# GpSimd takes the last two exponentials of a routed layer, and the first expert tile is prepared earlier

## The chip, the cores and the metric

The kernel runs on one core of a Trainium2 chip. The metric is the device time in microseconds (us) of the whole program, as the median of a few executions.

## What is computed

The input is two sequences of 2048 tokens, 256 numbers each. Two layers follow each other, both behind a layer normalisation and both added to their input:

```python
x = x + attn(layernorm(x))   # linear attention with decay, 4 heads, scanned in chunks
x = x + ffn(layernorm(x))    # 8 experts, each token goes to its 2 best
# inside ffn
logits = einsum('bsd,ed->bse', x, gate_w)
probs = softmax(logits)
topk_probs, topk_idx = top_k(probs, 2)
h = gelu(w1[expert] @ x + b1[expert])
y = w2[expert] @ h + b2[expert]
out = sum(y * topk_probs)
```

The softmax is computed as e to the logits less the largest, divided by its sum. The first step of that, for the last two of 16 chunks, is what the change touches.

## The kernel before

Each engine has one instruction stream, written out by hand, and they meet through semaphores. Work comes in two stages.

**Stage one** goes over 16 chunks of 128 tokens of both sequences at once (`m` = 0 to 15, `NCH` = 16). A step `n` handles several chunks, each at its own lag: loads and statistics of chunk n, attention of n-1 and n-2, residual sum and second normalisation of n-3, the experts' scores of n-4, and the routing of n-5. The routing of a chunk m on VectorE is:

- `logits(m)` copies the scores from PSUM; `largest(m)` takes the maxima and writes the shifted logits (`shifted`, 128 partitions by 16 numbers, semaphore `shifted_done`), then the indices; `choose(m)` makes the mask of the two best.
- ScalarE's `exponential(m)` turns `shifted` into its exponential in place (line 591, `exp_done`).
- `weigh_gates(m)` (lines 818 and 820) waits for it, sums it and masks it. `place(m)` (lines 826 to 844) finds each token's slot, with TensorE's `rank(m)`.
- GpSimd then sends the 128 rows of each of 2 sequences and 2 choices to the experts' lists in DRAM, by four indirect DMAs (line 501). It also computes the two normalisations' 1/sqrt, as a power of -0.5 over 128x2 (line 491).

**Stage two** goes over tiles of 256 or 128 tokens of one expert. The first four tiles start before all chunks are routed. A tile's rows are loaded by SyncE (line 429), turned by VectorE (`turn`, line 1133) and split into a high and a low half-precision part (`high_tile` on ScalarE, line 584; `low_tile` on VectorE, line 1140). `prepare(i)` on VectorE reads the tile's expert number into a register and copies that expert's bias and the tokens' gates (lines 1108 to 1126). TensorE runs `pair(f, z)`: group f of the first product (line 1518) interleaved with group z of the second (lines 1533 and 1535). Between them ScalarE's `gelu(g)` (line 737) and VectorE's `split(g)` (lines 1146 and 1148) work on a group. `gelu` of a tile's first group waits for its `prepare`. `finish(i)` (lines 1156 and 1161) weighs a tile's output, and GpSimd adds it to DRAM (line 532).

At the seam between the stages the last three chunks (13, 14, 15) are routed between the first groups. VectorE's order there is: turn(1), largest and choose(13), prepare(0), weigh_gates(13), residual(15) with its statistics (lines 851 to 866), split(0), place(13), low_tile(1), logits, largest and choose(14), split(1), weigh_gates(14), prepare(1), split(2), place(14), split(3), logits, largest and choose(15), split(4), turn(2), weigh_gates(15), place(15), split(5), low_tile(2), and then tables of tiles (`count_wide`, `table_wide`, ..., lines 1036 to 1104) among further splits. ScalarE's order is: exponential(13), gelu(0), the copy normed_transposed(14) (line 576), gelu(1), high_tile(1), gelu(2), normalise(15), exponential(14), gelu(3), normed_transposed(15), gelu(4), exponential(15), gelu(5) and so on. TensorE's is: pair(0), the turning of chunk 14, project(15) (line 1338), pair(1), rank(13), score_experts(14) (line 1349), pair(2), pair(3, 0), rank(14), the turning of chunk 15, pair(4, 1), score_experts(15), pair(5, 2), rank(15) and further pairs. Exponential and GELU need different tables on ScalarE, which are loaded by an instruction of its own in front of the first use (ACT_TABLE_LOAD).

Of the kernel before, what the change touches and what calls it, by code (L numbers as in the profile page):

```python
# [27 lines left out]
ALU = mybir.AluOpType  # L28
# [3 lines left out]
P = 128  # L32
B, T, D = 2, 2048, 256
H, HD = 4, 64
E, F = 8, 1024
# [75 lines left out]
def build(nc, x, w_write, w_read, decay, log_alpha, gate_w, experts, b1, b2, const, out):  # L111
    with ExitStack() as ctx:
        def sb(name, shape, dt=F32):
            return ctx.enter_context(nc.sbuf_tensor(name, shape, dt))
# [30 lines left out]
        decayC = sb("decayC", [P, KD])  # L145
        b1T = sb("b1T", [P, E, MF])
        minus_half = sb("minus_half", [P, 1])
        warm = sb("warm", [P, 1])
        zcol = sb("zcol", [P, B * KD, 1])
        base = sb("base", [P, E])  # L150
# [62 lines left out]
        def small(w, dt=F32):  # L213
# [62 lines left out]
            "x1_done", "stats2_done", "moments2_done", "ve2_done", "rs2_done", "shift2_done", "xm_done",  # L276
            "mT_ps", "mT_done", "logit_ps", "logit_done", "top_done", "top_at_done", "shifted_done", "exp_done",
            "pick_done", "mask_done", "esum_done", "rsum_done", "masked_done", "rank_ps", "slots_done",
            "picked_done", "slot_i_done", "base_done", "gates_done", "token_done", "whi_done", "wlo_done")}
        early_done = sem("early_done")  # L280
        wide_done = sem("wide_done")
        half_done = sem("half_done")
# [13 lines left out]
        def active(n, lag):  # L296

            return 0 <= n - lag < NCH

        def reached(eng, name, n):  # L300

            if n >= 0:
                eng.wait_ge(S[name], n + 1)
# [160 lines left out]
        @block.gpsimd  # L464
        def _(pool):
            pool.memset(minus_half[:], -0.5).then_inc(setup_pool, 1)
            pool.memset(zcol[:], 0.0)
            pool.memset(state[:], 0.0)
            last = pool.memset(readsT[:, 0, :, :, 0:1], 0.0)
            last.then_inc(setup_pool, 1)  # L470
            pool.memset(zrow, 0.0).then_inc(setup_pool, 1)
            pool.memset(pad[:], 0.0).then_inc(setup_pool, 1)
            pool.wait_ge(setup_pool, 1)

            def step(n):

                par = n % 2
                for lag, moments, ve, rs, shift, got, mid, end, last, used, ago in (
                        (0, moments1, ve1, rs1[par], shift1[par], "moments1_done", "ve1_done", "rs1_done",
                         "shift1_done", "res_done", 1),  # L480
                        (3, moments2, ve2, rs2, shift2, "moments2_done", "ve2_done", "rs2_done", "shift2_done",
                         "xm_done", 0)):
                    if active(n, lag):

                        m = n - lag
                        reached(pool, got, m)
                        reached(pool, used, m - ago - 1)
                        pool.tensor_scalar(ve, moments[:, :, 1], EPS, None, ALU.add)  # L488
                        pool.tensor_scalar(shift, moments[:, :, 0], -1.0, None, ALU.mult).then_inc(S[mid], 1)
                        reached(pool, mid, m)  # L490
                        pool.tensor_tensor(rs, ve, minus_half[:].to_broadcast([P, B]), ALU.pow).then_inc(S[end], 1)  # L491
                        reached(pool, end, m)
                        pool.tensor_tensor(shift, shift, rs, ALU.mult).then_inc(S[last], 1)
                if active(n, 5):
                    m = n - 5
                    for name in ("token_done", "xm_done", "gates_done", "slot_i_done"):
                        reached(pool, name, m)
                    for b in range(B):
                        for k in range(2):
                            at_bk = slot_i[:, m % ROWS, 2 * b + k:2 * b + k + 1]  # L500
                            pool.indirect_dma_start(  # L501
                                out=sent, out_offset=bass.IndirectOffsetOnAxis(ap=at_bk, axis=0),
                                in_=row[:, m % ROWS, b, :], in_offset=None).then_inc(row_out[m % ROWS], 16)
                if n == 2:

                    pool.wait_ge(setup_pool, 4)
                    pool.wait_ge(setup_dve, 14)
                    pool.wait_ge(padrow_done, 1)
                    for c in range(2):
                        pool.indirect_dma_start(  # L510
                            out=sent, out_offset=bass.IndirectOffsetOnAxis(ap=padrow_i[:, c:c + 1], axis=0),
                            in_=pad[:, c, :], in_offset=None).then_inc(pad_sent, 16)

            stage_one(step, 0)

            for n in range(NCH + 2, NCH + LAG):
                step(n)

            def add(i):

                if i == 0:
                    pool.wait_ge(x1_out[0], 16 * 6)
                    pool.wait_ge(x1_out[1], 16 * 5)
                if i == NE:
                    stored(pool)
                in_tile(pool, i)
                if i > 0:
                    pool.wait_ge(added, 16 * UNIT[i])
                for u in units(i):
                    came(pool, "ybias_done", u)  # L530
                    at_u = tile_in[:, u % 8, E:E + 1].bitcast(I32)
                    pool.indirect_dma_start(  # L532
                        out=out, out_offset=bass.IndirectOffsetOnAxis(ap=at_u, axis=0),
                        in_=yout[:, u % 4], in_offset=None, compute_op=ALU.add).then_inc(added, 16)

            for i in range(NT):
                add(i)
            pool.wait_ge(added, 16 * UNIT[NT])

        @block.scalar  # L540
        def _(a):
# [46 lines left out]
            def exponential(m):  # L588

                reached(a, "shifted_done", m)  # L590
                a.activation(shifted, shifted, ACT.Exp).then_inc(S["exp_done"], 1)
# [156 lines left out]
                                 scale=gate_cur[:, u % 8:u % 8 + 1]).then_inc(S2["yout_done"], 1)  # L748

            exponential(NCH - 3)  # L750
            gelu(0)
            normed_transposed(NCH - 2)
            gelu(1)
            high_tile(1)
            gelu(2)
            normalise(NCH - 1)
            exponential(NCH - 2)
            gelu(3)
            normed_transposed(NCH - 1)
            gelu(4)  # L760
            exponential(NCH - 1)
            for g in range(5, NG + 3):
                if g < NG:
                    gelu(g)
# [7 lines left out]
        def _(v):  # L772
# [41 lines left out]

            def weigh_gates(m):

                reached(v, "exp_done", m)
                v.tensor_reduce(esum, shifted, AX.X, ALU.add).then_inc(S["esum_done"], 1)
                reached(v, "mask_done", m)
                v.tensor_tensor(masked, shifted, mask[:], ALU.mult).then_inc(S["masked_done"], 1)  # L820
# [307 lines left out]
            def turn(i):  # L1128

                v.wait_ge(rows_ld[i % 2], 16 * NQ * (i // 2 + 1))  # L1130
                came(v, "tlo_done", i - 1)
                w = slice(0, KD * rows_of(i))
                v.transpose(tileT[:, w], tile_rows[:, i % 2, w]).then_inc(S2["turned_done"], 1)  # L1133
# [123 lines left out]
                split_low(j)  # L1257
            stage_one(step, 3)
            m = NCH - 3
            turn(1)  # L1260
            largest(m)
            choose(m)
            prepare(0)
            weigh_gates(m)
            residual(NCH - 1)
            residual_stats(NCH - 1)
# [326 lines left out]
```

## Time and profile before

| what | value |
|---|---|
| runs | 570.34 us, median of 3 (569.34 to 570.93) |
| profiled execution, first to last instruction | 576.6 us |
| TensorE busy | 534.6 us, 93% |
| VectorE busy | 457.3 us, 79% |
| ScalarE busy | 332.8 us, 58% |
| GpSimd busy | 244.5 us, 42% |
| mean granted clock of TensorE | 0.980 |

The profiled execution has no time of its own beside its span in what is at hand, so the span stands for both. In the views an engine is called PE (TensorE), DVE (VectorE), ACT (ScalarE), POOL (GpSimd) or SPq (SyncE's queue). A line such as L591 is line 591 of the kernel. In a timeline a row gives the start, the duration, the engine, the line, the operation with what it writes and reads, how many instructions are merged in it, and in brackets how long the engine was idle before it and what ended that. The busy shares are means over two stages with different limits; the seam lies between 160 and 226 us.

### The profile page before, as it was taken

What the parts mean: (1) busy time and instruction counts of PE and PEld (TensorE: products, weight loads), DVE (VectorE), ACT (ScalarE), POOL (GpSimd) and SP (SyncE); (2) the same over time, 40 slices, a digit from 0 to 9 for tenths busy, and PEclk for the clock granted to TensorE, in tenths of its full rate; (3) what the DMA queues carried; (4) which work ended last, traced back from release to release, by engine and by line L of the source; (5) the groups of instructions that cost most, each with busy time, mean ns of one, the idle gap of its engine ahead of it and who ended that gap; (6) DMA issues with size and microseconds to landing.
All of it is one profiled execution on the core that took longest, in us unless ns stands there. A gap on an engine that the chain in (4) does not pass through costs nothing.

```text
span 576.6 us, 17660 instructions
## 1 busy us (share of the span) xinstructions
PE 534.6 (93%) x5246; PEld 418.7 (73%) x5246; DVE 457.3 (79%) x1408; ACT 332.8 (58%) x841; POOL 244.5 (42%) x275
## 2 busy tenths in 40 slices
PE   7799889899988888999999999999999999999991
PEld 7677777777776656777777777777777777777770
DVE  5889999999976789777887877777777887877771
ACT  5899989888744633444545444544454545444540
POOL 2426778888846532432333222333332333222333
PEclk8999999999998979999999999999999999999996
DMA  5577767667334353444444344444444433444432
GB/s 162 199 221 224 254 205 214 188 216 215 122 96 123 113 179 58 78 71 68 67 65 62 63 70 75 78 75 75 70 71 67 68 62 62 65 69 76 76 48 27
DMA packets 85097, 63.34 MB, mean 110 GB/s; under 512 B 54224, under 2 KB 77392, under 8 KB 85008
## 3 DMA queue, kind: packets, MB, share of 16 engines
q1 hardware_dynamic: 71328, 43.94, 31.0%
q0 software_dynamic: 13392, 18.27, 17.1%
q8 instruction: 49, 0.80, 0.6%
q14 instruction: 40, 0.33, 0.2%
q10 hardware_dynamic: 288, 0.00, 0.0%
HBM read 37.56 MB, written 24.62 MB: 108 GB/s over the span
## 4 chain that ended last, share of the span: by engine, by line
PE 63%; DVE 13%; POOL 8%; issue 8%; ACT 3%; SPq 1%; DMA 1%; another core or an unknown queue 0%; ACTq 0%; DVEq 0%; POOLq 0%
PE psum L1518 29%; PE psum L1533 20%; PE psum L1535 10%; POOL sent_rows L501 4%; DVE weights L779 2%; POOL tiny L491 2%; POOL tiny L488 1%; DVE arena L915 1%; SPq L429 1%; PE psum L1338 1%; DVE tiny L858 1%; DMA arena<-in_x 1%; DVE tiny L881 1%; DVE arena L1146 1%; DVE arena L851 1%
## 5 line engine op out<-in xcount | busy, mean ns | idle before, releaser
L1518 PE MATMUL psum<-arena,weights 128*128 128x256 f16 (+1 forms) x2208 | 281.4, 250 | 4.3 <-issue 4.3
L1518 PEld LDWEIGHTS psum<-arena,weights 128*128 x2208 | 188.8, 99 | 83.1 <-issue 6.6
L737 ACT ACTIVATE arena<-psum,b_cur 128x256 f32<-128x256 f32 (+1 forms) x368 | 131.7, 423 | 159.9 <-PE psum L1518 120.4
L532 POOL DMA_INDIRECT out<-arena,tile_in x71 | 115.0, 1620 | 251.6 <-DVE arena L1161 150.3
L1533 PE MATMUL psum<-weights,arena 128*128 x568 | 215.7, 381 | 2.1 <-DVE arena L1148 2.1
L1535 PE MATMUL psum<-weights,arena 128*128 x568 | 155.4, 274 | 0.0
L1148 DVE TENSOR_TENSOR arena<-arena 128x512 f16<-128x512 f32 x142 | 99.6, 701 | 4.9
L501 POOL DMA_INDIRECT sent_rows<-arena,tiny x64 | 65.3, 1021 | 27.3 <-issue 16.6
L1146 DVE CAST arena<-arena 128x512 f16<-128x512 f32 x142 | 61.8, 435 | 6.1 <-ACT arena L737 5.8
L1533 PEld LDWEIGHTS psum<-weights,arena 128*128 128x128 f16 x568 | 55.8, 98 | 8.7 <-issue 2.6
L1535 PEld LDWEIGHTS psum<-weights,arena 128*128 128x128 f16 x568 | 55.8, 98 | 4.8
L1156 DVE SCALAR_TENSOR_TENSOR arena<-psum,gate_scaled,arena 128x256 f32<-128x256 f32 x71 | 32.0, 480 | 30.0 <-PE psum L1535 25.6
L1133 DVE STREAM_TRANSPOSE tileT<-arena 128x512 f32<-128x512 f32 (+1 forms) x46 | 26.8, 583 | 34.6 <-DMA arena<-sent_rows 34.6
L584 ACT ACTIVATE arena<-tileT 128x512 f16<-128x512 f32 (+1 forms) x46 | 24.5, 533 | 31.2 <-DVE tileT L1133 29.2
L779 DVE SCALAR_TENSOR_TENSOR weights<-weights 128x1024 f16<-128x1024 f32 x32 | 38.5, 1214 | 1.8 <-ACT weights L569 1.8
L1338 PE MATMUL psum<-wrT,arena 128*128 128x256 f32 x128 | 31.7, 391 | 8.8 <-ACT arena L643 8.8
L569 ACT ACTIVATE weights<-weights 128x1024 f16<-128x1024 f32 x32 | 34.2, 1070 | 0.0
L1338 PEld LDWEIGHTS psum<-wrT,arena 128*128 128x128 f32 x128 | 23.0, 189 | 14.6 <-ACT arena L643 12.1
L747 ACT ACTIVATE arena<-arena,gate_cur 128x256 f32<-128x256 f32 x71 | 33.2, 508 | 0.0
L1161 DVE SCALAR_TENSOR_TENSOR arena<-psum,gate_scaled,arena 128x256 f32<-128x256 f32 x71 | 31.8, 477 | 0.8
L488 POOL TENSOR_SCALAR tiny<-tiny 128x2 f32<-128x2 f32 x32 | 13.5, 422 | 37.8 <-DVE tiny L789 21.1
L491 POOL TENSOR_TENSOR tiny<-tiny,minus_half 128x2 f32<-128x2 f32 x32 | 25.5, 797 | 2.7
(172 smaller groups left out, 641.8 us busy)
## 6 DMA issues: line engine op xcount, KB each, us to landing
weights<-in_experts SPq DMA_DIRECT2D x32, 512.0 KB
arena<-sent_rows SPq DMA_DIRECT2D x100, 64.0 KB
arena<-in_b SPq DMA_DIRECT2D x46, 128.0 KB
arena<-in_x SPq DMA_DIRECT2D x16, 256.0 KB, 3.7
out<-arena SPq DMA_DIRECT2D x16, 256.0 KB, 4.1
arena<-sent_rows SPq DMA_DIRECT2D x84, 32.0 KB
sent_rows<-pad SPq DMA_DIRECT2D x7, 265.0 KB
tile_in<-sent_rows SPq DMA_DIRECT2D x71, 4.5 KB
```

The source lines that it names most:

```text
L491: pool.tensor_tensor(rs, ve, minus_half[:].to_broadcast([P, B]), ALU.pow).then_inc(S[end], 1)
L501: pool.indirect_dma_start(out=sent, out_offset=bass.IndirectOffsetOnAxis(ap=at_bk, axis=0), in_=row[:, m % ROWS, b, :], in_offset=None).th ...
L532: pool.indirect_dma_start(out=out, out_offset=bass.IndirectOffsetOnAxis(ap=at_u, axis=0), in_=yout[:, u % 4], in_offset=None, compute_op=A ...
L569: a.activation(halves[:, j * 2 * PIECE:j * 2 * PIECE + PIECE], weights[:, (j + AHEAD) * PIECE:(j + AHEAD + 1) * PIECE], ACT.Copy, scale=WS ...
L737: last = a.activation(act[:, g % 2, m * n:(m + 1) * n], ps_h[:, g % 2, m * n:(m + 1) * n], ACT.Gelu_apprx_tanh, scale=1.0 / WSCALE, bias=b ...
L779: v.scalar_tensor_tensor(out=halves[:, j * 2 * PIECE + PIECE:(j + 1) * 2 * PIECE], in0=weights[:, (j + AHEAD) * PIECE:(j + AHEAD + 1) * PI ...
L1146: v.tensor_copy(h_hi[:, g % 4], act[:, g % 2]).then_inc(S2["hhi_done"], 1)
L1148: v.tensor_tensor(h_lo[:, g % 4], act[:, g % 2], h_hi[:, g % 4], ALU.subtract).then_inc(S2["split_done"], 1)
L1338: last = pe.matmul(ps_proj[:, b], readsT[:, s, b, k, 0:P], wrT[:, k], start=(k == 0), stop=(k == KD - 1))
L1518: last = pe.matmul(ps_h[:, f % 2, mm * n:(mm + 1) * n], w1_of(e_of[i], k, lo, per * (f - GROUP[i]) + mm), turned[:, i % 2, part, k, 0:n], ...
L1533: pe.matmul(to, h_hi[:, z % 4, at], w2_of(e_of[t], m), start=(m == 0), stop=(m == MF - 1), skip_group_check=True)
L1535: last = pe.matmul(to[:, 0], h_lo[:, z % 4, at], w2_of(e_of[t], m)[:, 0], start=False, stop=(m == MF - 1), skip_group_check=True)
```

## The change

GpSimd gets a column `euler` that holds e, and a function `power(m)`, which writes e to the power of `shifted` over `shifted`, for m = 14 and 15. It stands in steps 18 and 19 of GpSimd's stream, in front of the indirect DMAs of chunk 13 and chunk 14. ScalarE's `exponential(14)` and `exponential(15)` are gone, and weigh_gates waits for `late_exp_done` in these two chunks. Behind exponential(13) ScalarE runs one small GELU on a column of zeros, so that its table is loaded there. On VectorE prepare(0) stands ahead of turn(1), not behind choose(13).

```diff
+        euler = sb("euler", [P, 1])
...
+            pool.memset(euler[:], float(np.e)).then_inc(setup_pool, 1)
             pool.wait_ge(setup_pool, 1)
+
+            def power(m):
+
+                if m == NCH - 2:
+                    pool.wait_ge(setup_pool, 5)
+                reached(pool, "shifted_done", m)
+                pool.tensor_tensor(shifted.rearrange("p b e -> p (b e)"), euler[:].to_broadcast([P, B * E]),
+                                   shifted.rearrange("p b e -> p (b e)"), ALU.pow).then_inc(S["late_exp_done"], 1)
...
+                if n >= NCH + 2 and active(n, 4):
+                    power(n - 4)
                 if active(n, 5):
                     m = n - 5
...
             exponential(NCH - 3)
+            a.activation(warm[:], zcol[:, 0], ACT.Gelu_apprx_tanh)
             gelu(0)
...
             normalise(NCH - 1)
-            exponential(NCH - 2)
             gelu(3)
             normed_transposed(NCH - 1)
             gelu(4)
-            exponential(NCH - 1)
...
-                reached(v, "exp_done", m)
+                if m < NCH - 2:
+                    reached(v, "exp_done", m)
+                else:
+                    v.wait_ge(S["late_exp_done"], m - NCH + 3)
...
             m = NCH - 3
+            prepare(0)
             turn(1)
             largest(m)
             choose(m)
-            prepare(0)
             weigh_gates(m)
```

## Rows read from the trace of the kernel before

**Rows 1.** Busy time in three stretches: us, busy (instructions), clock, DMA share, GB/s.

```profile
core 0: us, PE busy (x) PEld busy (x) DVE busy (x) ACT busy (x) POOL busy (x), PEclk, DMA share, GB/s
182.00:186.00 4.00, 4.00 (x22) 2.94 (x23) 3.73 (x21) 1.36 (x4) 3.06 (x5) 0.58 0.54 132
203.00:226.00 23.00, 19.83 (x131) 13.60 (x132) 21.39 (x77) 8.09 (x19) 7.15 (x5) 0.86 0.55 137
226.00:566.00 340.00, 338.18 (x3080) 258.53 (x3077) 263.02 (x644) 168.22 (x449) 105.09 (x65) 1.00 0.43 68
```

**Rows 2.** Timeline of VectorE at the seam, 175 to 204 us.

```profile
175.06 0.71 DVE L1133 STREAM_TRANSPOSE tileT<-arena 128x512 f32<-128x512 f32 x1 [1.89 <-DMA arena<-sent_rows]
...
176.71 0.17 DVE L813 TENSOR_TENSOR mask<-pick 128x16 bf16<-128x16 f32 x1
...
178.33 0.16 DVE L818 TENSOR_REDUCE tiny<-tiny 128x2 f32<-128x16 f32 x1
...
179.24 0.69 DVE L851 TENSOR_TENSOR arena<-psum,arena 128x512 f32<-128x512 f32 x1 [0.66 <-PE psum L1338]
...
183.28 0.16 DVE L873 COPY tiny<-psum 128x16 f32<-128x16 f32 x1
...
183.74 0.17 DVE L799 TENSOR_TENSOR tiny<-tiny 128x16 f32<-128x16 f32 x1
...
185.21 0.69 DVE L1148 TENSOR_TENSOR arena<-arena 128x512 f16<-128x512 f32 x1
...
188.36 0.17 DVE L818 TENSOR_REDUCE tiny<-tiny 128x2 f32<-128x16 f32 x1 [2.45 <-ACT tiny L591]
...
193.15 0.17 DVE L873 COPY tiny<-psum 128x16 f32<-128x16 f32 x1
...
196.19 0.13 DVE L818 TENSOR_REDUCE tiny<-tiny 128x2 f32<-128x16 f32 x1
...
196.95 0.42 DVE L1146 CAST arena<-arena 128x512 f16<-128x512 f32 x1
...
203.13 0.88 DVE L1156 SCALAR_TENSOR_TENSOR arena<-psum,gate_scaled,arena 128x256 f32<-128x256 f32 x2 [2.98 <-remote]
```

**Rows 3.** Groups of ScalarE by line: its table loads in stage two.

```profile
L737 ACT ACT_TABLE_LOAD x3 | 3.8, 1283 | 2.1 <-issue 2.1
...
L591 ACT ACT_TABLE_LOAD x2 | 2.6, 1283 | 0.0
```

**Rows 4.** Timeline of ScalarE, the first exponential of the seam and gelu(0)'s table.

```profile
176.20 0.22 ACT L591 ACTIVATE tiny<-tiny 128x16 f32<-128x16 f32 x1 [0.89 <-DVE tiny L799]
178.48 1.28 ACT L737 ACT_TABLE_LOAD   x1 [2.07 <-issue]
```

**Rows 5.** Timeline of TensorE (PEld: weight loads): the two scorings, and matmuls behind the first.

```profile
181.16 1.22 PE L1349 MATMUL psum<-gateT,arena 128*128 128x8 f32 x8 [0.88 <-ACT arena L576]
182.23 3.29 PE L1518 MATMUL psum<-arena,weights 128*128 128x256 f16 x15
...
191.01 0.97 PEld L1349 LDWEIGHTS psum<-gateT,arena 128*128 128x128 f32 x8 [0.41 <-ACT arena L576]
```

**Rows 6.** Timeline of GpSimd: first and last scatter of chunk 13, last of chunk 15.

```profile
183.88 1.08 POOL L501 DMA_INDIRECT sent_rows<-arena,tiny  x1 [0.47 <-issue]
...
188.31 0.96 POOL L501 DMA_INDIRECT sent_rows<-arena,tiny  x1 [0.30 <-issue]
...
202.36 0.96 POOL L501 DMA_INDIRECT sent_rows<-arena,tiny  x1 [0.30 <-issue]
```

**Rows 7.** GpSimd's power and multiply over 128x2: duration min/median/max in ns.

```profile
L491 POOL TENSOR_TENSOR tiny<-tiny,minus_half x32: 707/718/1602, 6.9 to 182.3; 128x2 f32<-128x2 f32 x32
...
L493 POOL TENSOR_TENSOR tiny<-tiny x32: 193/206/1142, 7.7 to 183.1; 128x2 f32<-128x2 f32 x32
```

**Rows 8.** Timeline of SyncE: issue of the rows of tile 4.

```profile
216.89 1.88 SPq L429 DMA_DIRECT2D arena<-sent_rows  x4
```

**Rows 9.** Timeline of VectorE and GpSimd around 56 us.

```profile
56.09 1.21 DVE L779 SCALAR_TENSOR_TENSOR weights<-weights 128x1024 f16<-128x1024 f32 x1
...
56.30 1.59 POOL L491 TENSOR_TENSOR tiny<-tiny,minus_half 128x2 f32<-128x2 f32 x1
```

More of the change, by code:

```diff
@@ L278, in build @@
             "pick_done", "mask_done", "esum_done", "rsum_done", "masked_done", "rank_ps", "slots_done",
-            "picked_done", "slot_i_done", "base_done", "gates_done", "token_done", "whi_done", "wlo_done")}
+            "picked_done", "slot_i_done", "base_done", "gates_done", "token_done", "whi_done", "wlo_done", "late_exp_done")}
         early_done = sem("early_done")
```

## The prediction

> **What bounds the kernel now.** I read the page first, then the windows, then the timelines of the engines between 174 and 226 us. From 226 us on TensorE is the bound: busy 338.18 of 340 us at full clock, with VectorE at 263 [rows 1]. Nothing of the change lies there, so it can move the end only by moving the point at which that stretch begins. Ahead of it, from 203 to 226 us, VectorE is busy 21.39 of 23 us [rows 1]: the routing tables, splits and finishes are one queue, and TensorE waits for it. What VectorE gains or loses before split(5), which starts at 196.95 [rows 2], should therefore arrive at the end in full, if nothing else stops it in between. The one large stop behind that point is at 203.13, where it has been idle for 2.98 us on something that the trace calls remote [rows 2].
>
> Between 175 and 197 us VectorE waits in three places that matter: 1.89 us for the rows of tile 1 before turn(1), 0.66 us before residual(15) for TensorE, and 2.45 us before weigh_gates(14), which starts at 188.36, for ScalarE's exponential [rows 2]. The last wait is the one that the change is about: the shifted logits of chunk 14 had been ready since 183.74 + 0.17 = 183.91 [rows 2], but ahead of their exponential in ScalarE's queue stood gelu(2), normalise(15) and a table load.
>
> **The change, part by part.** *Table loads.* After stage one starts to hand over, ScalarE does five loads of 1283 ns, two in front of exponentials and three in front of GELUs [rows 3]. Behind the change one is left, brought forward by the small activation on `warm`. Four go: 4 x 1.283 = 5.1 us of ScalarE, and two activations. ScalarE isn't the bound, so this isn't a gain by itself. It ends earlier what others wait for.
>
> *prepare(0).* It costs VectorE 1.45 us, from the end of choose(13) at 176.71 + 0.17 = 176.88 to weigh_gates(13) at 178.33. In its new place it falls into the 1.89 us idle before turn(1) [rows 2], which waits for a DMA, and is hidden with 0.4 us to spare. Were that cover gone, it would cost 1.45 us once more. It gates gelu(0), whose table load starts at 178.48 [rows 4]. Now the last exponential ends at 176.20 + 0.22 = 176.42, the table follows to 177.7, and gelu(0) can start near 178.0 instead of 178.48 + 1.28 = 179.76. VectorE doesn't gain at once: residual(15) at 179.24 waits for TensorE's projection, and everything from there to logits(14) at 183.28 is solid work [rows 2]. TensorE does gain. It was idle 0.88 us before score_experts(14) for the copy behind gelu(0), and right behind it 15 matmuls took 3.29 us [rows 5] while the granted clock of that stretch was 0.58 [rows 1]. So TensorE gets ahead by 0.9 us, or by up to 2.3 if the clock stays up: 3.29 us at 0.58 would be some 1.9 us at 1, so 1.4 us more.
>
> *The wait of weigh_gates(14).* GpSimd is free at 183.88 - 0.47 = 183.41 [rows 6], so power(14) starts when the logits are there, at 183.96, and ends at 183.96 + D, where D is the time of a power over 128x16. VectorE reaches the wait when split(1) is done, at 185.21 + 0.69 = 185.90 [rows 2]. weigh_gates(14) starts at the later of the two, instead of at 188.36. Behind it in VectorE's queue stand prepare(1), split(2), place(14), split(3) and logits(15), 4.79 us up to 193.15 [rows 2]. Everything that TensorE and ScalarE wait for hangs on them.
>
> *D.* The trace shows the power only over 128x2, at a median of 718 ns, and beside it a multiply of the same shape at 206 ns [rows 7]. If the half microsecond between them is paid once per instruction, D is 0.72 us. If it is paid per element, D is 0.2 + 8 x 0.52 = 4.4 us. The nearest row is the power itself, and with one width alone it fits both ends equally well. So I take the middle, 2.5 us, and keep both ends.
>
> *Scatters.* The two powers are put in front of the four indirect DMAs of the chunk before. Those of chunk 13 take from 183.88 to 188.31 + 0.96 = 189.27, 5.39 us [rows 6]. Behind the change they start after power(14), and power(15) stands behind them. So power(15) can't start before 183.96 + D + 5.45.
>
> *The sum, at D = 2.5.* power(14) ends at 186.46 and weigh_gates(14) runs 1.9 us earlier than now. logits(15) comes at 186.46 + 4.79 = 191.25. It also needs TensorE's scores of chunk 15. Their weight loads ended at 191.01 + 0.97 = 191.98, behind 0.41 us idle for ScalarE [rows 5], and move forward by that and by TensorE's 0.9 to 2.3 us, to between 189.3 and 190.7; that doesn't bind here. From logits(15) to weigh_gates(15) VectorE has 196.19 - 193.15 = 3.04 us of work [rows 2], so it is ready at 194.29. GpSimd ends the scatters of chunk 13 at 191.9, power(15) at 194.4 and the wait ends at 194.5. From there to split(5) it is 0.76 us [rows 2], so split(5) starts at 195.25 instead of 196.95: 1.7 us earlier. In general it starts at 190.25 + 2D once D is over about 2. Below that the scores of chunk 15 bind, or VectorE's own queue (185.90 + 4.79 = 190.7, less what the register load of prepare(1) overlaps), and the gain stays between 193.15 - 190.7 = 2.5 and 193.15 - 189.3 = 3.9 us. It is zero at D = 3.35.
>
> *What is late next.* The scatters of chunks 14 and 15 now end near 194.4 + 2 x 5.3 = 205.0 instead of 202.36 + 0.96 = 203.32 [rows 6]. SyncE waits for them before the rows of tile 4, issued at 216.89 [rows 8]; that hides the 1.7 us. The additions of tile 0 on the same queue start no later than now by more than that, and their buffers are wanted again only two tiles later. Without this cover it would cost the 1.7 us.
>
> The profiled execution spans 576.6 us, 6.3 more than the median of the runs, 570.34. I make the sum as a difference and take it off the median: 570.34 - 1.7 = 568.6 us. The stop at 203.13 and the low clock behind it may be part of those 6.3 us.
>
> **A shared port.** At 56.30 us a power took 1.59 us, while VectorE ran an operation with two inputs in SBUF from 56.09 to 57.30 [rows 9]; the usual is 0.72 [rows 7]. So the power can be held up by VectorE, by 0.87 us there. power(14) now meets split(1), and power(15) meets split(4), whose second halves of 0.69 us have two such inputs [rows 2]. Each power can so grow by up to 0.69 us, and the chain holds both: the gain of 1.7 shrinks to 0.3.
>
> The Trainium skill, SBUF — State Buffer, "Who interferes with whom", says that a VectorE instruction with two SBUF inputs contends with a GpSimd instruction that reads SBUF, and that the one that comes second is blocked outright. The trace agrees for a power that comes second: 1.59 us. By that rule the result would be that of the rival (C) below, 570.0; by the sum it is 568.6.
>
> **The rivals.** *(A) The power scales with its elements, D = 4.4.* For it: the power costs 3.5 times a multiply of the same shape, so most of its time is its own arithmetic [rows 7]. Against it: with two elements some of that may be paid once for all. split(5) would start at 190.25 + 8.8 = 199.05, 2.1 us later: 572.4 us, slower. It decides from D = 3.35 on, and by more than the measurement can tell from D = 4.2 on. *(B) The power is cheap, D under 2.* The gain is held at 2.5 to 3.9 us, in the middle 3.2, by TensorE's scores of chunk 15 and VectorE's own work: 567.1 us. *(C) The port.* Both powers are held up: 570.0, no change. For it speaks the row at 56.30, against it that the median power took 0.72 [rows 7]. *(D) The stop at 203.13 stays where it is.* If it doesn't move with the work before it, it swallows what was gained: 570.3. It ends within 0.4 us of the last scatter's end, at 203.32 [rows 2, 6]; if that is its cause, the later scatters make it 1.7 us later, 572.0. Against it: ScalarE and VectorE both wait there for TensorE's counts, not for a DMA.
>
> **How the numbers follow.** Chances: my forecast (D from 2 to 3, no port) 0.37, the cheap power (B) 0.20, the power by elements (A) 0.20, the port (C) 0.12, the stop at 203.13 (D) 0.11. The likeliest gives 568.6, with a range of its own of 567.6 to 569.6 for D half a microsecond either way. The wide range goes from 566.4, the best case of (B) at 570.34 - 3.9, to 572.4, case (A). A measurement of this kernel can tell about 0.3%, 1.7 us, from no change. My forecast lies right on that bound. I give it 0.25 faster and 0.12 same; with (B) faster is 0.45. (C) and 0.08 of (D) are no change, 0.20 together, so with my 0.12 same is 0.32. (A) and the other 0.03 of (D) make slower 0.23.
>
> **What would show it.** One load of 1.28 us on ScalarE near 176.4 and none later; gelu(0) near 178; prepare(0) just ahead of turn(1), and turn(1) still at 175.1. A power of 128x16 of some 2.5 us on GpSimd, with weigh_gates(14) released by it near 186.5 and the second power behind the scatters of chunk 13. The wait of weigh_gates(15), nothing now, should be small. The gain is there if split(5) starts 1 to 3 us earlier, and if TensorE still has the same lead near 226. The prediction is wrong if the power takes over 3.35 us or under 2, if turn(1) slips behind prepare(0), or if VectorE's stop near 203 grows by what was gained.

## The result, and the profile after

| | before | changed |
|---|---|---|
| median of 20 runs each, us | 569.33 (567.90 to 572.98) | 571.39 (569.23 to 575.49) |
| ratio, 95% interval | | 1.0032, 1.0017 to 1.0047 |
| profiled execution, its own time, us | none at hand; span 576.6 | 573.81; span 572.0 |
| VectorE busy / ScalarE / GpSimd, us | 457.3 / 332.8 / 244.5 | 457.8 / 327.3 / 248.5 |

The changed kernel is slower by 2.06 us between the medians, by 1.8 us if the ratio is taken (its interval reaches from 1.0 to 2.7 us). The forecast was 1.7 us faster. The time lies in the range, and the sign is wrong. The changed kernel's profile spans 4.6 us less than the one of before although its runs take longer. So the two traces can't be compared by their ends, and that is the first thing to be cleared up below.

The page of the changed kernel, span and busy time of each engine:

```profile
span 572.0 us, 17659 instructions
PE 534.5 (93%) x5246; PEld 419.9 (73%) x5246; DVE 457.8 (80%) x1408; ACT 327.3 (57%) x836; POOL 248.5 (43%) x278
```

ScalarE's groups by line, all table loads of stage two in the changed kernel, against [rows 3]:

```profile
L763 ACT ACT_TABLE_LOAD x1 | 1.3, 1283 | 0.0
```

Five loads became one, and ScalarE lost the 5.1 us of work that the prediction takes off (332.8 - 327.3 = 5.5 with the two activations). The timeline of ScalarE shows the load right behind exponential(13), ahead of gelu(0), against [rows 4]:

```profile
173.82 0.22 ACT L603 ACTIVATE tiny<-tiny 128x16 f32<-128x16 f32 x1
174.05 1.28 ACT L763 ACT_TABLE_LOAD   x1
175.35 0.20 ACT L763 ACTIVATE warm<-zcol 128x1 f32<-128x1 f32 x1
175.46 0.82 ACT L749 ACTIVATE arena<-psum,b_cur 128x256 f32<-128x256 f32 x2
```

VectorE's timeline of the changed kernel answers to [rows 2]. In order: turn(1), residual(15), split(1)'s second half, weigh_gates(14), weigh_gates(15), split(5), and the first finish:

```profile
171.97 0.71 DVE L1147 STREAM_TRANSPOSE tileT<-arena 128x512 f32<-128x512 f32 x1 [0.50 <-DMA arena<-sent_rows]
...
177.29 0.69 DVE L865 TENSOR_TENSOR arena<-psum,arena 128x512 f32<-128x512 f32 x1 [2.98 <-PE psum L1352]
...
183.07 0.69 DVE L1162 TENSOR_TENSOR arena<-arena 128x512 f16<-128x512 f32 x1
...
185.06 0.17 DVE L832 TENSOR_REDUCE tiny<-tiny 128x2 f32<-128x16 f32 x1 [1.30 <-POOL tiny L482]
...
193.59 0.17 DVE L832 TENSOR_REDUCE tiny<-tiny 128x2 f32<-128x16 f32 x1 [0.79 <-POOL tiny L482]
...
194.39 0.62 DVE L1160 CAST arena<-arena 128x512 f16<-128x512 f32 x1
...
197.81 0.88 DVE L1170 SCALAR_TENSOR_TENSOR arena<-psum,gate_scaled,arena 128x256 f32<-128x256 f32 x2
```

Two waits for GpSimd, 1.30 and 0.79 us, stand where the kernel before had the one wait of 2.45 us for ScalarE. The finish at 197.81 waits for nothing, where the one of before stood 2.98 us [rows 2].

GpSimd's timeline of the changed kernel, its two powers and the scatters of chunk 13 between them, against [rows 6, 7]:

```profile
182.12 2.90 POOL L482 TENSOR_TENSOR tiny<-euler,tiny 128x16 f32<-128x16 f32 x1 [0.66 <-DVE tiny L810]
185.20 1.07 POOL L513 DMA_INDIRECT sent_rows<-arena,tiny  x1 [0.17 <-issue]
...
189.11 1.48 POOL L513 DMA_INDIRECT sent_rows<-arena,tiny  x1 [0.31 <-issue]
190.62 2.93 POOL L482 TENSOR_TENSOR tiny<-euler,tiny 128x16 f32<-128x16 f32 x1
193.75 1.04 POOL L513 DMA_INDIRECT sent_rows<-arena,tiny  x1 [0.19 <-issue]
```

The first power ends at 182.12 + 2.90 = 185.02, and weigh_gates(14) starts 0.04 us later. The second starts as soon as the last scatter of chunk 13 is issued, and VectorE starts 0.04 us behind its end, too. So the chain of the prediction is there: power, scatters, power. It remains to be found what it has to be held against.

The windows are those of [rows 1], moved by the 4 us by which the changed trace is ahead in its second and third row:

```profile
core 0: us, PE busy (x) PEld busy (x) DVE busy (x) ACT busy (x) POOL busy (x), PEclk, DMA share, GB/s
182.00:186.00 4.00, 4.00 (x37) 3.15 (x36) 1.91 (x9) 2.05 (x5) 3.70 (x2) 1.00 0.51 91
199.00:222.00 23.00, 17.34 (x116) 11.62 (x115) 21.48 (x77) 6.73 (x16) 10.63 (x9) 0.93 0.72 164
222.00:562.00 340.00, 337.78 (x3075) 257.95 (x3073) 262.19 (x642) 168.22 (x449) 106.00 (x66) 1.00 0.43 67
```

The last row is the steady stretch: TensorE's busy time there is that of before within half a microsecond, the other engines' within one. The first shows a clock of 1.00 where the trace of before had 0.58. That this is no work of the change is shown by the next runs.

### The profile page after: what moved, and what is told of

It reads as the page before. It is cut to its first block, busy times and chain, and to the rows that moved or that the text cites. A ratio compares the mean times of both kernels' runs of the same rounds, so it can differ in the third digit from the quotient of the medians.

```text
span 572.0 us, 17659 instructions
## 1 busy us (share of the span) xinstructions
PE 534.5 (93%) x5246; PEld 419.9 (73%) x5246; DVE 457.8 (80%) x1408; ACT 327.3 (57%) x836; POOL 248.5 (43%) x278
## 4 chain that ended last, share of the span: by engine, by line
PE 74%; DVE 12%; issue 5%; POOL 3%; ACT 3%; DMA 1%; SPq 0%; DVEq 0%; ACTq 0%; POOLq 0%
PE psum L1532 30%; PE psum L1547 20%; PE psum L1549 10%; PE psum L1352 3%; PE psum L1442 2%; PE psum L1435 2%; PE psum L1416 2%; POOL sent_rows L513 1%; DVE arena L929 1%; PE psum L1363 1%; DVE weights L790 1%; PE psum L1402 1%; PE psum L1455 1%; DMA arena<-in_x 1%; ACT arena L613 1%
## 5 line engine op out<-in xcount | busy, mean ns | idle before, releaser
L498 POOL TENSOR_SCALAR tiny<-tiny 128x2 f32<-128x2 f32 x32 | 10.4, 324 | 37.7 <-DVE tiny L800 20.7
```

## The experiments

Landmarks are read on VectorE's timeline and counted from the start of residual(15), the first instruction behind the seam's own wait for TensorE. That takes out what differs ahead of the seam. From split(12) to the end of the execution the traces need 351.4 to 352.2 us, all but that of k10 (353.0), so what a kernel gains or loses at split(12) is gained or lost for good.

| trace | weigh_gates(14) | weigh_gates(15) | split(5) | split(12) | runs: ratio (95%) |
|---|---|---|---|---|---|
| before, as shown ahead | 9.12 | 16.95 | 17.71 | 45.54 | |
| changed | 7.77 | 16.30 | 17.10 | 42.54 | 1.0032 (1.0017 to 1.0047) |
| k1 before, again | 7.02 | 15.21 | 17.92 | 42.87 | 1.0006 (0.9980 to 1.0032) |
| k2 prepare(0) alone | 6.99 | 14.47 | 16.21 | 42.46 | 0.9984 (0.9960 to 1.0007) |
| k3 powers alone | 7.75 | 16.55 | 17.36 | 42.87 | 1.0030 (0.9999 to 1.0061) |
| k4 multiply for power | 6.38 | 14.70 | 15.47 | 44.27 | 1.0042 (1.0017 to 1.0066) |
| k5 before, column added | 6.99 | 14.47 | 15.23 | 40.37 | 1.0018 (1.0000 to 1.0037) |
| k6 changed, column last | 7.75 | 16.15 | 16.95 | 42.52 | 1.0049 (1.0027 to 1.0071) |
| k7 multiply on VectorE | 6.79 | 14.17 | 15.00 | 39.92 | 0.9987 (0.9966 to 1.0009) |
| k8 changed, again | 7.76 | 16.15 | 16.95 | 42.57 | 1.0036 (1.0017 to 1.0055) |
| k9 multiply, column last | 6.39 | 13.36 | 14.12 | 39.56 | 0.9964 (0.9941 to 0.9987) |
| k10 half power | 6.50 | 14.15 | 14.91 | 40.16 | 0.9988 (0.9968 to 1.0008) |
| k11 power twice | 10.62 | 21.87 | 22.67 | 48.10 | 1.0130 (1.0106 to 1.0154) |
| k12 prepare(0) alone, again | 6.99 | 14.46 | 15.22 | 40.35 | 0.9993 (0.9970 to 1.0016) |
| k13 multiply, column in place | 6.39 | 13.36 | 14.13 | 39.57 | 0.9984 (0.9966 to 1.0002) |
| k14 multiply, column last | 6.38 | 13.35 | 14.11 | 39.57 | 0.9979 (0.9963 to 0.9996) |
| k15 changed, again | 7.76 | 16.28 | 17.08 | 42.68 | 1.0041 (1.0023 to 1.0059) |

The runs came in four lots, each on a chip of its own with the kernel before beside it (so a chip can't be told from the hour in which it was used): k1 to k4 (median of before 578.18 us), k5 to k8 (569.00), k9 to k12 (569.15), k13 to k15 (568.71). The ratios are always to the runs of before on the same chip. A ratio is not exactly the quotient of two medians: the medians give 8.0 us for k11 where the ratio gives 7.4. Differences of runs are taken from the ratios below, unless medians are named. In k4, k7, k9, k13 and k14 a product with e stands in place of the exponential, and in k10 only the first sequence's logits are raised, so that the gates of those chunks are other numbers; everything else is computed as before.

### First lot: the halves of the change

**k1, the kernel before once more.** Is the trace of before a usual one?

> The kernel before, unchanged, as a control. All theories: the time is the same within 0.3%. What its trace is for: in the trace of before that I predicted from, VectorE stood still 2.98 us at 203.13 and TensorE ran at half clock twice at the seam (182 to 185 and 203 to 209 us). If that was one execution's bad luck, the 2.98 us stop is gone here and the time from turn(1) to split(5), 21.9 us there, is 20.5 us or less, so that my base for the sum was too slow. If it belongs to the kernel, both are here again.

It took 578.18 us with 12 runs, as the runs beside it did, 9 us more than before took elsewhere. So this chip is slower for every kernel. The span of the trace shown ahead, 576.6, falls between the spans of this lot (576.1 to 581.1). With the 1.8 us that lie around a span elsewhere (573.81 - 572.0) it makes 578.4, which no one of the 20 runs of before reached (572.98 at most). In this trace weigh_gates(14) starts 7.02 us behind residual(15), not 9.12. So the long wait of the forecast isn't usual even on this chip. This trace has stops of the remote kind as well: ScalarE or VectorE stands still on something that the trace calls remote, where the program has it wait for TensorE's count. (They are called late counts from here on.) They stand at other places. The longest behind residual(15), in ScalarE's timeline:

```profile
198.39 0.84 ACT L737 ACTIVATE arena<-psum,b_cur 128x256 f32<-128x256 f32 x2 [2.54 <-remote]
```

**k2, prepare(0) and the small activation alone.**

```diff
+            a.activation(warm[:], zcol[:, 0], ACT.Gelu_apprx_tanh)
...
+            prepare(0)
             turn(1)
...
-            prepare(0)
```

> Only prepare(0) ahead of turn(1), with the small GELU behind exponential(13); the exponentials of chunks 14 and 15 stay on ScalarE. Theory 1 (the two powers of 2.9 us each on the chain cost what the change lost): this half is harmless, 0 to 1.5 us faster than before, and 2 us or more faster than the changed kernel. Theory 2 (TensorE gets to the table stretch early, idles, and loses its clock): this half alone is already 1 us or more slower than before.

0.9984, and 0.9993 on another chip (k12). Neither can be told from 1.

**k3, the powers alone,** without moving prepare(0): the changed kernel with that one call in its old place.

> Only the powers on GpSimd, prepare(0) at its old place. Theory 1 (the powers): as slow as the changed kernel or slower, 1.5 to 3 us over before, with weigh_gates(14) and weigh_gates(15) released by the power. Theory 2 (early TensorE): nearer to before, within 1 us, since TensorE is not early.

1.0030, near the changed kernel's own ratio, though its interval reaches down to 0.9999. That points at the powers and not at the move, but doesn't show it: at split(12) this trace stands where that of k1 does, 42.87. The length series below is what shows it.

**k4, a cheap operation in the power's place,** with the same waits and the same position in GpSimd's queue.

```diff
-                                   shifted.rearrange("p b e -> p (b e)"), ALU.pow).then_inc(S["late_exp_done"], 1)
+                                   shifted.rearrange("p b e -> p (b e)"), ALU.mult).then_inc(S["late_exp_done"], 1)
```

> The changed kernel with a multiply in place of the power on GpSimd, so that the gates are other numbers but every instruction, wait and DMA stays. The operation should take 0.2 to 0.4 us instead of 2.9. Theory 1: the two waits on GpSimd vanish, split(5) comes 2 to 3 us earlier after turn(1), and the time is 1.5 to 4 us under before. Theory 2: the time stays within 1 us of before or above, because VectorE's tables bound the stretch after it and TensorE's clock drops in its gaps.

This ran against me: 1.0042, slower with an operation of 0.22 us. It could mean that the length of the power is beside the point. Up to split(5) the trace says the opposite, 15.47 against 17.10, and then it loses all of that and more in late counts, as the timeline of all engines of k4 has them:

```profile
205.32 0.84 ACT L749 ACTIVATE arena<-psum,b_cur 128x256 f32<-128x256 f32 x2 [4.16 <-remote]
...
207.54 0.88 DVE L1170 SCALAR_TENSOR_TENSOR arena<-psum,gate_scaled,arena 128x256 f32<-128x256 f32 x2 [3.91 <-remote]
```

Three explanations were open besides the first, the length of the powers (theory 1): that TensorE, fed earlier, is granted less clock (theory 2); that the new column shifts the addresses of all that is declared behind it (theory 3); that the place on GpSimd costs, whatever runs there (theory 4). A fifth came later, that k4's result was its chip's.

### Second lot: the column, and the place

**k5, the kernel before with the column `euler` declared and not used.**

```diff
+        euler = sb("euler", [P, 1])
```

> The kernel before with the new column euler declared behind minus_half and nothing else, so that every buffer declared after it (the arena, tileT, the small ones) lies 4 bytes further in each partition. Theory 3 (the addresses): the shift alone costs what the change lost, 1.5 us or more over before. Theories 1 and 2, and a theory 4 (GpSimd's queue: its place in the chain, not the power's length, costs): no difference within 0.2%.

1.0018, an interval that begins at 1.0000. By itself it settles nothing. Its trace is the one that mattered most: the kernel before without a late count anywhere at the seam. VectorE's timeline of k5, with residual(15), weigh_gates(14), weigh_gates(15) and split(5):

```profile
176.29 0.69 DVE L852 TENSOR_TENSOR arena<-psum,arena 128x512 f32<-128x512 f32 x1 [1.91 <-PE psum L1339]
...
183.28 0.17 DVE L819 TENSOR_REDUCE tiny<-tiny 128x2 f32<-128x16 f32 x1 [0.25 <-ACT tiny L592]
...
190.76 0.13 DVE L819 TENSOR_REDUCE tiny<-tiny 128x2 f32<-128x16 f32 x1
...
191.52 0.42 DVE L1147 CAST arena<-arena 128x512 f16<-128x512 f32 x1
```

The wait of weigh_gates(14) for ScalarE's exponential is 0.25 us, not 2.45, and split(5) starts 191.52 - 176.29 = 15.23 us behind residual(15), not 17.71. It is 0.25 us in k12, too, and 0.28 in k1, a trace of the kernel before itself:

```profile
184.37 0.17 DVE L819 TENSOR_REDUCE tiny<-tiny 128x2 f32<-128x16 f32 x1 [0.25 <-ACT tiny L591]
```

```profile
188.36 0.17 DVE L818 TENSOR_REDUCE tiny<-tiny 128x2 f32<-128x16 f32 x1 [0.28 <-issue]
```

ScalarE's timeline of k5 shows why: gelu(2), normalise(15), the load and the exponential follow each other without a gap.

```profile
179.91 0.84 ACT L738 ACTIVATE arena<-psum,b_cur 128x256 f32<-128x256 f32 x2 [0.95 <-PE psum L1519]
180.64 1.08 ACT L602 ACTIVATE arena<-arena,tiny 128x256 f32<-128x256 f32 x2
181.74 1.28 ACT L592 ACT_TABLE_LOAD   x1
183.03 0.22 ACT L592 ACTIVATE tiny<-tiny 128x16 f32<-128x16 f32 x1
```

TensorE's timeline holds what came before. The 15 matmuls of group 2 took 3.29 us in the trace of before [rows 5], and in k5:

```profile
178.40 1.80 PE L1519 MATMUL psum<-arena,weights 128*128 128x256 f16 x15
```

**k6, the changed kernel with the column declared last,** so that no other address moves.

```diff
-        euler = sb("euler", [P, 1])
...
+        euler = sb("euler", [P, 1])   # behind every other buffer
```

> The changed kernel with the column declared last, so that every other buffer keeps the address that it has before. Theory 3: the loss goes, the time is that of before or up to 1 us under it. Theory 4: as slow as the changed kernel, 1.5 to 2.5 us over before.

1.0049, as slow as the changed kernel. The addresses are not it.

**k7, the multiply on VectorE,** in its own queue ahead of weigh_gates(14) and (15): neither ScalarE's exponential nor GpSimd.

```diff
-                if n >= NCH + 2 and active(n, 4):
-                    power(n - 4)
...
+                    v.tensor_tensor(shifted.rearrange("p b e -> p (b e)"), euler[:].to_broadcast([P, B * E]),
+                                    shifted.rearrange("p b e -> p (b e)"), ALU.mult).then_inc(S["late_exp_done"], 1)
```

> The changed kernel with the column last, and in place of GpSimd's power a multiply on VectorE itself, right before it sums (the gates are other numbers). No engine but VectorE takes part, and GpSimd's scatters have nothing in front of them. Theory 4 (GpSimd's place): faster than before by 1 to 3 us, and faster than the multiply on GpSimd by 3 us or more. Theory 2 (being early at the tables is worth nothing): within 0.5 us of before or slower. Theory 3: like the preceding run or a little faster.

0.9987, no change that can be told. Even with the exponentials of these chunks taken off ScalarE for 0.17 us of VectorE each, split(5) comes at 15.00 instead of 15.23. That is 0.23 us, where the forecast saw 2.5 to 3.9 for a cheap operation. It isn't the ceiling of the idea: the multiply on GpSimd reaches 14.12 below (k9).

**k8, the changed kernel again.**

> The changed kernel, unchanged, on the chip of the other runs. All theories: 1.5 to 2.5 us over before (ratio 1.002 to 1.005). Its trace is for comparison: if the late counts of TensorE that all traces of this chip show at the seam are absent, as in the trace of the changed kernel from the other chip, they belong to the kernel; if they are there, to the chip.

1.0036. The loss repeats, with the landmarks of k6. The clock of theory 2 doesn't carry it: over all runs the mean granted clock of the changed kernel is 0.987 here and in k15, and 0.985 in k6, and that of the kernel before beside them is 0.984 to 0.985. The changed kernel is slower at no lower clock.

### Third lot: a series over the length

**k9, k4's multiply with the column last.**

> The changed kernel with a multiply in place of the power on GpSimd (the gates are other numbers), now with the column last. Theory 1 again, with the base mended (in a trace of before without late counts, split(5) starts 15.2 us after residual(15), and with the power 11.0 + 2D, D its length): the operation takes 0.2 us, split(5) starts near 15.0, and the time is 0 to 0.8 us under before. Theory 4 (being in GpSimd's queue costs, whatever the length): 2 us over before, as the first run of this edit had it (1.0042).

0.9964, against k4's 1.0042, and the interval is below 1. split(5) starts at 14.12, 1.1 us ahead of k5, though k5's wait for the exponential was only 0.25 us. VectorE's timeline of k9, with weigh_gates(14) and the first copy of prepare(1), and of k5, with that copy:

```profile
180.84 0.16 DVE L832 TENSOR_REDUCE tiny<-tiny 128x2 f32<-128x16 f32 x1
...
181.34 0.17 DVE L1124 COPY b_cur<-b1T 128x8 f32 x1 [0.25 <-issue]
```

```profile
184.39 0.17 DVE L1111 COPY b_cur<-b1T 128x8 f32 x1 [0.85 <-issue]
```

prepare(1) reads the tile's expert number into a register before that copy. The gap ahead of the copy is 0.85 us or more in each trace where weigh_gates(14) had to wait for another engine, however little (0.1 us in k10), and 0.25 in k4, k9, k13 and k14, where it had not; in k7 it is 0.49. So 0.6 of the 1.1 us go with there being a wait at all. The prediction only hints at this ("less what the register load of prepare(1) overlaps").

GpSimd's timeline of k9:

```profile
179.28 0.22 POOL L482 TENSOR_TENSOR tiny<-euler,tiny 128x16 f32<-128x16 f32 x1 [0.66 <-DVE tiny L810]
...
185.71 0.23 POOL L482 TENSOR_TENSOR tiny<-euler,tiny 128x16 f32<-128x16 f32 x1
```

**k10, the power over half the numbers.**

```diff
-                pool.tensor_tensor(shifted.rearrange("p b e -> p (b e)"), euler[:].to_broadcast([P, B * E]),
-                                   shifted.rearrange("p b e -> p (b e)"), ALU.pow).then_inc(S["late_exp_done"], 1)
+                pool.tensor_tensor(shifted[:, 0], euler[:].to_broadcast([P, E]), shifted[:, 0],
+                                   ALU.pow).then_inc(S["late_exp_done"], 1)
```

> The power over one sequence's 8 numbers only, 128x8 (the other sequence's gates are other numbers). Between 718 ns for 2 and 2.9 us for 16 numbers a straight line gives 1.65 us. Theory 1: both waits on GpSimd are gone or under 0.2 us, split(5) is 15.0 to 15.3 us after residual(15), and the time is within 0.8 us of before, on either side. Theory 4: 2 us over before.

0.9988, on the level of before. GpSimd's timeline of k10:

```profile
181.28 1.64 POOL L482 TENSOR_TENSOR tiny<-euler,tiny 128x8 f32<-128x8 f32 x1 [0.65 <-DVE tiny L810]
...
188.52 1.67 POOL L482 TENSOR_TENSOR tiny<-euler,tiny 128x8 f32<-128x8 f32 x1
```

**k11, each power preceded by one more into a spare buffer.**

```diff
+                pool.tensor_tensor(twice[:], euler[:].to_broadcast([P, B * E]),
+                                   shifted.rearrange("p b e -> p (b e)"), ALU.pow)
                 pool.tensor_tensor(shifted.rearrange("p b e -> p (b e)"), euler[:].to_broadcast([P, B * E]),
```

> The changed kernel with a second power of 128x16 in front of each of the two, into a spare buffer; the gates are right. Theory 1: D is 5.8 us, split(5) starts 11.0 + 11.6 = 22.6 us after residual(15), 7.4 us later than before, and the time is 7.4 us over before (ratio 1.013). If the powers' cost isn't the chain's, it is far less: 2 us over before, as for one power (theory 4).

1.0130, which is 7.4 us (six runs). VectorE's timeline of k11 has both waits grown, and split(5) at 198.31 - 175.64 = 22.67:

```profile
175.64 0.69 DVE L868 TENSOR_TENSOR arena<-psum,arena 128x512 f32<-128x512 f32 x1 [2.55 <-PE psum L1355]
...
186.26 0.17 DVE L835 TENSOR_REDUCE tiny<-tiny 128x2 f32<-128x16 f32 x1 [4.15 <-POOL tiny L485]
...
197.51 0.17 DVE L835 TENSOR_REDUCE tiny<-tiny 128x2 f32<-128x16 f32 x1 [3.51 <-POOL tiny L485]
...
198.31 0.61 DVE L1163 CAST arena<-arena 128x512 f16<-128x512 f32 x1
```

**k12, k2 again.**

> Only prepare(0) ahead of turn(1), once more, for a trace and a time beside the others. Theory 1: 0 to 0.8 us under before, since VectorE still waits for TensorE's projection before residual(15) and for ScalarE's exponential by no more than 0.3 us. Theory 2: 1 us over.

Its landmarks are those of k5 to 0.02 us, with prepare(0) at the other place.

### Fourth lot: the multiply with both layouts

k4 and k9 differed in the column's place and in the chip. Here both layouts ran on one chip, with the changed kernel beside them.

> The multiply on GpSimd with the column where the change has it (the edit of the first call). Theory 5 (the chip was the cause): like the form with the column last beside it, within 0.2% of it, and 1 to 2 us under before if this chip shows no late counts. Theory 3 (the column's place): 1 us or more slower than that form.

> The multiply on GpSimd with the column last, as in the third call, beside the form before. Theory 5: both forms agree; 1 to 2 us under before on a chip without late counts, over before on one with them. Theory 3: this one is faster by 1 us or more.

> The changed kernel beside the two. Both theories: 1.5 to 2.5 us over before on a chip without late counts, and 3 to 4 us over the multiply, since the multiply takes 2.7 us less twice, of which the bound of VectorE's own queue leaves about 2 us at split(5) and the measured 1.9 + 2.0 us at the end.

0.9984 and 0.9979 with landmarks that agree to 0.02 us, and 1.0041 for the changed kernel. The layout makes no difference, and k4's kernel (k13 is the same) isn't slower here. With an operation of 0.22 us the same place in the same queue gives nothing or a small gain, and with 2.9 us it gives the loss.

Put in order of the time D that one operation takes on GpSimd, the series reads: 0.22 us 0.9964, 0.9984, 0.9979; 1.65 us 0.9988; 2.9 us 1.0032, 1.0049, 1.0036, 1.0041; 5.8 us 1.0130. k4 alone doesn't fit. Its 12 runs show the lowest mean clock of all kernels, 0.978 against 0.982 of before beside it.

## Why the prediction was wrong

**The loads and prepare(0).** Right. The load is at 174.05 instead of the 176.4 that it was put at, because all is earlier in this trace; what counts is that gelu(0) follows it at once. prepare(0) is covered by the wait for tile 1's rows, of which 0.50 us are left. It is worth nothing, since VectorE then stands longer for TensorE ahead of residual(15): 2.98 us here, 1.91 in k5, 0.66 in the trace of before [rows 2]. That TensorE "gets ahead by 0.9 us, or by up to 2.3 if the clock stays up" came to nothing: in k5 the 15 matmuls take 1.80 us without the move, as they do with it (1.80 at 179.40 in the changed trace).

**The step that failed** is the base of the gain: "weigh_gates(14) starts at the later of the two, instead of at 188.36", with the wait of 2.45 us that "the change is about". That wait was not the kernel's but this one execution's: of the five traces with both exponentials on ScalarE (before, k1, k2, k5, k12) it alone has it. In [rows 1] the granted clock from 182 to 186 is 0.58, half speed for most of it, 15 matmuls take 3.29 us, and gelu(2), normalise(15) and the exponential behind them are late. Other traces have a stretch of low clock as well, but ahead of residual(15): from 170 to 174 us it was 0.76 in k5, 0.57 in k12 and 0.63 in the changed kernel. So where it falls differs from one execution to the next. In k5, k12 and k1 weigh_gates(14) starts 7.0 us behind residual(15), 2.1 earlier. The text did note that the profile spans 6.3 us more than the runs, and that the stop at 203.13 "and the low clock behind it may be part of those 6.3 us". It didn't ask whether the wait on which the whole gain rested was part of them as well. The right base was in its own sum: the bound that it gives for VectorE's own queue, logits(15) at 190.7, puts split(5) at 190.7 + 3.04 + 0.76 = 194.5, which is 15.3 behind residual(15). The usual kernel, at 15.23, stands on that bound already.

**The chain itself** was right. Counted from residual(15), at 179.24, the prediction's 190.25 + 2D for split(5) is 11.01 + 2D. For D = 2.9 that is 16.8 (measured 16.95 to 17.10), for D = 5.8 it is 22.6 (22.67). Held against the usual 15.23 and not 17.71, it gives a crossing at D = (15.23 - 11.01) / 2 = 2.1 us, not at 3.35. k10 at 1.65 us lies on the fast side of it, the changed kernel on the slow side. Under the crossing the formula no longer holds: it gives 14.3 for k10 and 11.5 for the multiply, which measured 14.91 and 14.12, since weigh_gates(14) and weigh_gates(15) then hardly wait for GpSimd and VectorE's own work sets the time.

**D** was mis-sized: 2.90 and 2.93 us measured, 2.5 taken, 2 x 0.4 = 0.8 us on the chain. With the right base the forecast's own D would have given 11.01 + 5.0 - 15.23 = 0.8 us slower, and the measured one gives 1.6. So the base decides the sign, and D half of the size.

**The sum.** split(5) is 1.7 to 1.9 us later than in k5 (k8 and the changed kernel), split(12) 2.2 us, and the medians of the runs 2.06. The further 0.3 to 0.5 us come between those two points, and 0.2 to 0.3 of them are no wait but split(5) itself: its cast takes 0.62 us in the changed kernel, with one of GpSimd's scatters being issued from 193.75 to 194.79, and 0.42 in k5 (191.52). A scatter is under way there too, so why the one cast is longer stays open. That a shift at split(5) arrives at the end was right, and k11 shows it best: 7.44 us at split(5), 7.7 at split(12), 7.4 in the runs by the ratio and 8.0 by the medians.

**The rivals.** (A), the power by its elements, was the nearest in its sign; the width series lies between the two bounds, 0.72 us at two numbers [rows 7], 1.64 at 8, 2.90 at 16, which is some 0.4 us once and 0.157 us a number. It would not have decided under the crossing of 3.35. That the measured time lies in the range is owed to this rival, whose 572.4 is the range's upper end, and not to the forecast of 568.6. (B), a cheap power with a gain of 2.5 to 3.9 us, was tried by the multiply: 0.9964, 0.9984 and 0.9979, which is 2.0, 0.9 and 1.2 us. (D) didn't occur: with nothing late there is no stop to move. (C), the port, didn't occur either, and is taken up below.

**What stays open.** Why the clock fell just there in the trace of before. Why TensorE's counts reach the other engines late in some executions, and why on the first lot's chip so often. Between 176 and 226 us late counts stand in the trace of before and in all four of the first lot, and in none of the other twelve traces. k4's 1.0042 may come from there or from its lower clock; one trace can't explain 12 runs, so its cause isn't shown. A version that beats both kernels was not found: the multiply computes other numbers, and moving prepare(0) alone gave 0.9984 and 0.9993, which can't be told from 1.

## What to carry to other kernels

Before a wait is taken as the kernel's, set the profiled execution's span against the runs; where it lies outside all of them, look for a clock dip or a late count ahead of that wait, and count on less than all of it. Work moved to another engine leaves one queue and enters another: here the operation stands twice in a chain with the four scatters between, so its length counts double, and one crossing length decides between gain and loss. If the length is not in the trace, the forecast is that crossing with a chance on either side, and the crossing deserves as much care as the length.

## What the runs showed of the hardware

GpSimd's power costs 0.72 us over 128x2, 1.64 over 128x8 and 2.90 over 128x16; a multiply with e over 128x16 took 0.22. The time grows with the width by itself, so one instruction over everything saves only some 0.4 us of it.

The port. In the changed kernel the power started first, at 182.12, and VectorE's operation with two inputs in SBUF ran inside it, at 183.07, in its usual 0.69 us; the power took 2.90, as in the 128x16 rows of k11, where the second one had no such neighbour. Nobody was held. A little earlier the order was the other way, in the timeline of all engines of the changed kernel:

```profile
179.47 0.69 DVE L1162 TENSOR_TENSOR arena<-arena 128x512 f16<-128x512 f32 x1
...
179.58 0.66 POOL L499 TENSOR_SCALAR tiny<-tiny 128x2 f32<-128x2 f32 x1
```

GpSimd came second, and an operation whose mean over its 32 executions is 235 ns took 0.66, to 180.24, 0.08 us behind the end of VectorE's at 180.16. The Trainium skill, SBUF — State Buffer, "Who interferes with whom", has such a pair contend for a port that whoever issues first holds for its whole instruction, with the other blocked (it says the blocking of VectorE's two-port modes, and calls the lock exclusive in general). The row at 179.58 agrees with it, as the one of [rows 9] does; the pair at 182.12 and 183.07 does not. What makes the difference, the order of the engines or the kind of operation, was not tried.

Chips differ more than these kernels do: the kernel before took 578.18 us on one chip and 569.15, 569.00 and 568.71 on three others, 1.6% apart, and a ratio taken beside it on the slow chip was contradicted on another (k4 and k13, the same kernel: 1.0042 and 0.9984).
